# ScalarE instead of VectorE writes the placing matrix (both layers) and the last-edge coefficients (layer 1)

## The reference, cut to what matters

```
h = relu(layernorm(x));  x = x + layer0(h)      # tensor products of h[src] with edge attributes, summed by dst
h = relu(layernorm(x));  x = x + layer1(h)
# layer1: c    = w_comp[etype]                      16 coefficients an edge
#         a    = tanh(relu(sum(x_hat * y_hat) / sqrt(32)))   attention of an edge
#         nei  = segment_sum(a * sum_b c_b * (h[src] @ weight_b), dst)
#         curr = h[src[last edge of the node]] @ self_loop_weight
#         relu(nei + curr)
```

## Time and profile before

| | us |
|---|---|
| median of 3 runs (3200.29 to 3203.24) | 3202.84 |
| the profiled execution, its own time | 3200.61 |
| its span, first to last instruction | 3198.8 |
| PE busy | 3075.6 (96%) |
| VectorE busy | 2687.4 (84%) |
| POOL busy | 2333.2 (73%) |
| ScalarE busy | 779.6 (24%) |

### The profile page before, as it was taken

One profiled execution on the slowest core, in us unless ns is written; L12 is line 12 of the kernel. 1 busy time (PEld: TensorE's weight loads), 2 busy tenths in 40 slices (PEclk: granted clock), 3 DMA queues, 4 the chain that ended last, 5 costly groups with the idle time before them and its releaser, 6 DMA issues.

```text
span 3198.8 us, 112293 instructions
## 1 busy us (share of the span) xinstructions
PE 3075.6 (96%) x44682; PEld 2741.8 (86%) x44682; DVE 2687.4 (84%) x4152; ACT 779.6 (24%) x1648; POOL 2333.2 (73%) x2461
## 2 busy tenths in 40 slices
PE   2999999999999999999699999999999999999998
PEld 2888888888888888888589989898988988999997
DVE  7777777777777777777589999999999999999996
ACT  2000000000000000000343434343433343333442
POOL 6777777777777777777477777777777777777774
PEclk9999999999999999999699999999999999999998
DMA  4111111111111111111233333333333333333232
GB/s 141 32 28 29 29 28 28 29 29 29 29 29 29 29 28 28 28 29 31 74 61 59 56 59 57 59 56 59 57 59 55 60 57 59 55 60 59 56 65 47
DMA packets 217720, 151.05 MB, mean 47 GB/s; under 512 B 121592, under 2 KB 198349, under 8 KB 217167
## 3 DMA queue, kind: packets, MB, share of 16 engines
q1 hardware_dynamic: 137999, 100.77, 12.7%
q0 software_dynamic: 78592, 40.40, 12.0%
q10 hardware_dynamic: 576, 2.40, 0.2%
HBM read 135.13 MB, written 8.22 MB: 45 GB/s over the span
## 4 chain that ended last, share of the span: by engine, by line
PE 75%; DVE 14%; issue 7%; DVEq 2%; ACT 1%; DMA 0%; ACTq 0%
PE ps L625 51%; PE ps L651 10%; PE ps L682 8%; DVE blocks L946 4%; PE ps L664 3%; DVE scratch L955 3%; DVE room L1025 2%; PE ps L638 2%; DVE dots L996 1%; DVE xg L960 1%; DVE squares L993 1%; PE ps L588 1%; DVEq L1038 1%; DVE squares L1033 1%; DVE coef L1006 1%
## 5 line engine op out<-in xcount | busy, mean ns | idle before, releaser
L553 POOL DMA_INDIRECT xg<-h_table,idx x2456 | 2322.4, 946 | 829.2 <-issue 712.9
L625 PE MATMUL ps<-h,blocks 128*128 128x448 f32 x9380 | 2048.3, 372 | 40.3 <-DVE blocks L946 37.2
L625 PEld LDWEIGHTS ps<-h,blocks 128*128 128x128 f32 x9380 | 1725.9, 188 | 202.6 <-issue 27.7
L946 DVE TENSOR_TENSOR blocks<-scratch,ps 128x896 fp32r<-128x896 int16 x670 | 722.2, 1078 | 16.6 <-issue 9.2
L1025 DVE TENSOR_TENSOR room<-coef,ps 128x756 f32<-128x756 f32 (+1 forms) x522 | 648.7, 1284 | 5.0 <-DVE ps L966 0.2
L955 DVE SCALAR_TENSOR_TENSOR scratch<-ramp_sb,scratch,ps 128x448 f32<-128x448 f32 x670 | 452.1, 675 | 172.7 <-PE ps L625 170.5
L819 ACT ACTIVATE p_left<-ps 32x168 f32<-32x168 f32 (+1 forms) x262 | 78.6, 300 | 1774.4 <-PE ps L682 1763.9
L682 PEld LDWEIGHTS ps<-room,xg 128*32 128x32 f32 x25008 | 370.6, 110 | 86.3 <-issue 75.5
L682 PE MATMUL ps<-room,xg 128*32 128x28 f32 (+3 forms) x25008 | 431.1, 209 | 14.0 <-issue 9.4
L960 DVE TENSOR_REDUCE xg<-scratch 128x32 f32<-128x448 f32 x670 | 415.5, 620 | 24.4
L651 PEld LDWEIGHTS ps<-w_sb,p_left 128*84 128x84 f32 (+1 forms) x2610 | 243.6, 153 | 28.0 <-ACT p_left L820 3.5
(11 more groups left out here) (102 smaller groups left out, 837.3 us busy)
## 6 DMA issues: line engine op xcount, KB each, us to landing
xg<-h_table,idx POOLq DMA_INDIRECT x2456
rows_b<-typ_short SPq DMA_DIRECT2D x130, 258.0 KB
scratch<-q_short SPq DMA_DIRECT2D x260, 96.0 KB
rows_b<-dst_short SPq DMA_DIRECT2D x130, 126.0 KB
coef<-in_edge_dram SPq DMA_DIRECT2D x130, 54.0 KB
att_tab<-p_table SPq DMA_DIRECT2D x393, 8.1 KB
p_table<-room SPq DMA_DIRECT2D x8, 297.0 KB, 3.6
X<-in_x_dram SPq DMA_DIRECT2D x7, 224.0 KB, 4.9
```

Of the source, the lines that this page charges most:

```text
L553: pool.indirect_dma_start(xg[:, g.q, t - g.s * J, :], None, h_table[n], bass.IndirectOffsetOnAxis(ap=idx[:, t:t + 1], axis=0)).then_inc(L. ...
L625: last = pe.matmul(found_ps[b], blocks[:, b, c, :], h_2[:, a, c], start=(c == 0 and a == 0), stop=(c == NCH - 1 and a == 1))
L946: dve.tensor_tensor(blocks[:, b], q_b[:, g.b, i, :].unsqueeze(1).broadcast_to([P, NCH, P]), block_ps.unsqueeze(2).broadcast_to([P, NCH, P] ...
```

## The change

ScalarE gets two new functions, and VectorE loses `last_edges` and the last part of `spread`. ScalarE writes `R` as it makes the one-hot rows: Abs of `place - n` for each of the two halves, then Relu of one minus that over both, in place, behind a wait on a new semaphore `off_set`. It does so at the end of step t for group t-1, and in layer 1 it copies the last-edge coefficients of group t just before. `iota_row` is the ramp in SBUF; VectorE had read it from PSUM (`iota_ps`). Some waits are added ahead of the loops on ScalarE, since `R` shares memory with the tile `squares`.

```
 # ScalarE, edge_copies
+                def last_edges(g):
+                    b, nj = g.b, g.nj
+                    tiles = slice(FULL * J, T) if g.tail else bass.ds(g.s * J, J)
+                    wait(act, L.Z_set, g.order() * 2 - 4)
+                    act.activation(coef1[:, b, 0:nj, NBASE], last_all[:, tiles], ACT.Copy).then_inc(L.last_set, 1)
+
+                def placing(g):
+                    hh, w = g.halves()
+                    wait(act, L.placed, g.order() - 2)
+                    for h in range(hh):
+                        at = place[0:w, FULL, h:h + 1] if g.tail else place[0:w, bass.ds(g.s, 1), h]
+                        act.activation(R[0:w, g.b, h, :], iota_row[0:w, :], ACT.Abs, bias=at, scale=-1.0)\
+                           .then_inc(L.off_set, 3 - hh)
+                    act.wait_ge(L.off_set, g.order() * 2)
+                    act.activation(R[0:w, g.b, 0:hh, :], R[0:w, g.b, 0:hh, :], ACT.Relu, bias=1.0, scale=-1.0).then_inc(L.R_set, 1)
...
                     if n == 1 and gs[1]:
                         attention(gs[1])
+                    if n == 1 and gs[0]:
+                        last_edges(gs[0])
+                    if gs[1]:
+                        placing(gs[1])
...
+            act.wait_ge(high_set, NCH)
+            act.wait_ge(consts_in, 16)
+            act.wait_ge(windows_set, 11)
             edge_copies(0)
...
+            act.wait_ge(high_set, 2 * NCH)
+            act.wait_ge(split_set, 2 * NCH)
             act.wait_ge(p_set, NU)
             edge_copies(1)
 # VectorE, edge_work
-                def last_edges(g):
-                    b, nj = g.b, g.nj
-                    wait(dve, L.Z_set, g.order() * 2 - 4)
-                    one = iota_ps[:, 1:2]
-                    dve.tensor_tensor(coef1[:, b, 0:nj, NBASE], tiles(last_all, g), one.broadcast_to([P, nj]), ALU.mult)\
-                       .then_inc(L.last_set, 1)
...
-                    hh, w = g.halves()
-                    wait(dve, L.placed, o - 2)
-                    at = place[0:w, FULL, 0:hh] if g.tail else place[0:w, bass.ds(g.s, 1), :].rearrange("p a h -> p (a h)")
-                    dve.tensor_tensor(R[0:w, b, 0:hh, :], at.unsqueeze(2).broadcast_to([w, hh, P]),
-                                      iota_ps[0:w].unsqueeze(1).broadcast_to([w, hh, P]), ALU.is_equal)\
-                       .then_inc(L.R_set, 1)
...
-                    if n == 1 and new:
-                        last_edges(new)
```

More of the change, by code:

```diff
@@ L377, in __init__ @@
                 self.Z_set = sem(f"Z_set{n}")
+                self.off_set = sem(f"off_set{n}")
                 self.R_set = sem(f"R_set{n}")
@@ L836, in step @@
                         attention(gs[1])
+                    if n == 1 and gs[0]:
+                        last_edges(gs[0])
+                    if gs[1]:
+                        placing(gs[1])
                 def one_pass(k):
-                    if n == 1 and not isinstance(k, int):
+                    if not isinstance(k, int):
                         act.wait_ge(L.moved_on, k * (2 + 2 * n))
```

## The result

The changed kernel takes 3186.08 us in the median of four runs (3184.47 to 3187.71), the kernel before 3201.57 us in four runs beside them (3200.19 to 3203.24): ratio 0.9951, 95% interval 0.9939 to 0.9963. The profiled execution took 3186.35 us (span 3184.4, clock 0.984), where that of before took 3200.61: 14.3 us less. Forecast were 13.8 us less (3186.8 us) for that execution and a median of 3189 us, in a range from 3181 to 3198.

A forecast was written before the change was run, and what follows sets the result against it. POOL was taken to bound layer 0 and PE layer 1, with VectorE close behind. 0 + 17.4 - 4.0 + 0.4 = 13.8 us off 3200.6 gave 3186.8, median 3189, range 3181 to 3198.

The forecast's parts named there:

- Layer 0, 0 us: Layer 0: POOL's gathers bound it and VectorE idles, so the lighter VectorE gains 0 us.
- Start of layer 1, 0.4 us: Start of layer 1: PE's 0.41 us of idle time there is given back, 0.4 us gained.
- Loop, 17.4 us of excess: Eight turns of VectorE's loop in layer 1: they exceed PE's own pace by 17.4 us, which a lighter VectorE can recover.
- The 10.1 us put down to small latenesses between the ends: Layer 1 loop, steps between turns' ends: 10.1 us of the excess, wiped out by 0.54 us less VectorE work a step.
- Of it 4.0 us stay at the turns' ends: Layer 1, seven turns' ends: PE's branch stalls of 7.3 us give back 3.3 us and 4.0 us stay.
- The predicted 0.47 us by which the branch moves up: Each turn's end in layer 1: the branch comes 0.47 us earlier, from 0.12 us of sequencer work and 0.35 us at L1006.
- ScalarE's 1.4 to 1.7 us in cover: ScalarE in layer 1: 1.4 to 1.7 us added a step, covered by 5.34 us idle before copy_G, costing nothing.
- The tails, 0 to 0.5 us: Ends of the layers: 0, at most 0.5 us lost each, where placing of group 130 stands before its copy_G.
- the rival with the free turn's end: Layer 1 turns' ends: the branch stalls vanish too because the turn gets shorter, gain 17.8 us, 3185 us; chance 0.32.
- The chain as the cause: Layer 1: find, project, copy_o, attention, L1006 and Z set the pace, not VectorE's load; gain 6 us, 3197; chance 0.15.
- further table load: ScalarE before Tanh: switching function tables each step costs 1.28 us a load, some 65 us in all, 3268; chance 0.05.
- The signs: Trace checks: layer 1's copy_G 1163 us apart, PE idle 2 to 5 us, layer 0's end within 0.5 us, VectorE 76 us less busy.

The follow-up runs named there:

- e3: Kernel before with ScalarE writing R in layer 0 only, layer 1 as before; 0.7 us of difference in the median against the kernel before.
- the load put back: Changed kernel with VectorE also doing its two old instructions into buffers nobody reads; 3195.80 us against 3203.83 for the kernel before, ratio 0.9976.
- e11: Kernel before with VectorE doing the is_equal of the placing matrix twice in both layers; 27 us more than the kernel before (+0.55%).
- the last experiment: The run with VectorE's two old instructions put back into the changed kernel, for nobody; 3195.80 us, ratio 0.9976 against the kernel before.
- e8: The full change once more, on a chip where the kernel before takes over 4700 us; ratio 0.9876 against the kernel before.
- e7: Changed kernel with three more copies on ScalarE per step of layer 1, 5.7 us a step; faster than the kernel before, ratio not in the text.
- e6: Changed kernel with the last-edge copy given back to VectorE, so only R is moved; its two runs gained 12 and 15 us against the kernel before.

## Why the prediction was right

*Layer 0, 0 us.* Right: POOL's rows didn't change. e3 adds less than it seems to, since POOL waits for PE there.

*Start of layer 1, 0.4 us.* `copy_G` of group 0 came 0.8 us earlier (1620.66 against 1621.47), but at group 10 only 0.1 us was left of it. No gain from here in the end.

*Loop, 17.4 us of excess.* Right, and now with a cause in VectorE's own step: 24.31 us a pair against PE's 24.15, plus the turns' ends. The 10.1 us put down to small latenesses between the ends were there: PE's stalls of over 0.2 us outside the seven turns' ends add up to 6.7 us before and 0.5 after, and the rest of the 10.1 us is not in stalls of that length. That the gain would be the excess and not the 52 us freed was right too. What the forecast didn't see is that the excess is the loop's own: written out, VectorE's two-tile step is 0.45 us shorter.

*Of it 4.0 us stay at the turns' ends.* This is the term that was mis-sized. PE's seven stalls were 7.7 us before (7.3 forecast) and 1.0 are left of them, not 4.0; the turns as a whole kept 1.3 us of excess. The place of the earlier trace rows, one turn's end, VectorE in the kernel after:

```profile
2019.41 0.36 DVE L1026 TENSOR_TENSOR coef<-ps,att 128x192 f32<-128x192 f32 x1 [0.22 <-ACT att L795]
2019.81 3.19 DVE L1045 TENSOR_TENSOR room<-coef,ps 128x1428 f32<-128x1428 f32 x2
2024.05 1.09 DVE L974 TENSOR_TENSOR blocks<-scratch,ps 128x896 fp32r<-128x896 int16 x1 [1.05 <-issue]
```

The chain of waits there, kernel after:

```profile
2019.89 0.06 DVEq L179
...
2023.81 0.09 DVEq L179
```

and PE behind it:

```profile
2025.19 0.47 PE L626 MATMUL ps<-h,blocks 128*128 128x448 f32 x1 [0.60 <-DVE blocks L974]
```

From the branch to the sequencer's next instruction it is 3.92 us, before 4.29. Over the seven turns of layer 1 the mean fell from 3.94 to 3.43 us. The predicted 0.47 us by which the branch moves up came (it stood 0.98 us behind the end of the attention and stands 0.51 behind it), and 0.51 us of fetch came off as well: 7 x 0.98 = 6.9 us of the 7.3, and PE's wait here fell from 1.43 to 0.60 us. I had taken the fetch as fixed. With the load put back it is 3.90 us again. The number of VectorE's records in a turn is 529, 480 and 528 in the three kernels, so it goes with the length here (469 were forecast for the change); on the other chips it doesn't (2.82 to 2.92 us at 480 to 541 records, and 3.29 in layer 0 of e11 at 454). Why is open.

*ScalarE's 1.4 to 1.7 us in cover.* Right: Abs 0.39 us (0.38 forecast), Relu 0.42, copy 0.22 (0.20). The idle time ahead of `copy_G` in the step of the earlier trace rows went from 5.34 us to 4.11, L1026 waits for ScalarE's attention as foreseen, and PE doesn't wait for ScalarE in the turns. The rule of the Trainium skill that was weighed ("ScalarE: Activation LUTs", "Rules for kernel authors": relu and add go to VectorE) holds for the busy time, which more than doubled for the same values; the measured ratio says that it doesn't decide where ScalarE idles.

*The tails, 0 to 0.5 us.* Too small, and for another reason than the one forecast. Group 128 still comes 15.8 us ahead of before; then 1.4 us are lost between `copy_G` and `copy_o` of group 129, in PE's 20 matmuls of `project`. Busy time in this stretch (columns as in the earlier trace rows), first the kernel before,

```profile
3171.30:3174.40 3.10, 2.02 (x20) 1.79 (x20) 0.00 (x0) 0.96 (x3) 0.00 (x0) 1.00 0.00 0
```

then the kernel after.

```profile
3155.60:3160.00 4.40, 3.42 (x20) 3.09 (x20) 0.00 (x0) 0.90 (x2) 0.00 (x0) 0.50 0.00 0
```

The granted clock (the column before the last two) is 1.00 before and 0.50 after, that is 2.4 and 1.2 GHz, and the same 20 matmuls take 3.42 us instead of 2.02. Both kernels had fallen to the lower clock a little before, each in an idle time of PE of over 1 us: the kernel before at 3167.7 us, ahead of the `sum_edges` that starts at 3168.02, the kernel after at 3149.9, ahead of the `attention_rows` that starts at 3150.55, some 2 us earlier in its tail. The kernel before had the full clock again from 3171.1 to 3174.5 us, which is this stretch, the kernel after never. What decided that was not tried. `placing` of group 130, which the forecast had named, comes only behind.

*The sum.* Forecast 13.8; measured in the profiled executions 0.1 (to group 10) + 16.1 (turns) - 0.4 (to group 127) - 1.5 (tail) = 14.3. Two errors of opposite sign, 2.7 us in the turns and 1.5 us in the tail, nearly cancel, so that the sum comes within 0.5 us is luck in part. The median was forecast as 3189 and is 3186.08: the 2.2 us by which the median before lay over its profiled execution were carried over, and the kernel after has its median 0.3 us below. The 3185 of the rival with the free turn's end is thus nearer than the forecast's own 3189.

*The rivals.* That the turn's end comes free nearly came true in its time, but not for its reason. Its evidence was misread: "shows no stall from the branch" in layer 0 is not so. The branch at 592.1 is followed by the sequencer's next instruction at 594.99, and L946 starts 0.24 us behind that, at 595.23, just as in layer 1 (2027.75 and 2027.98). The 0.86 us of idle time ahead of it are the end of a fetch, though the row names PE as the releaser, and the same holds at all seven turns' ends of that layer. The fetch takes 2.87 us there in the mean (2.82 after); it costs nothing since VectorE has time to spare in layer 0. The fetch did not end at 480 records a turn either, where the page "Advanced Engine Details and Errata", section "ISA Cache", of the Trainium skill gives room for 512 instructions; the trace doesn't bear out a limit at 512 recorded instructions. The chain as the cause fell with the last experiment. No further table load was seen: there is one within the layers' edges, as before.

*The signs.* The two `copy_G` stand 1160.6 us apart (1163 forecast), PE idles 2.0 us in the turns (2 to 5), and layer 0 ends 0.3 us later (within 0.5). VectorE's busy time in layer 1 fell by 59 us, from 1467.7 to 1408.4, and not by 76.

## What to carry to other kernels

Measure each engine's own period over the repeating pattern of steps, from a point that doesn't wait to the next. Where an engine's period is a little above the bounding engine's, work taken off it is worth the difference, times the number of periods, and nothing beyond; it may cost more than twice the time on an engine that idles. A branch at the end of a turn is a term of its own, and how much of it shows depends on how long an instruction covers it. Compare the same step inside and outside a hardware loop too: here the loop's register work made VectorE the slower engine.

## What the runs showed of the hardware

- The kernel before takes 3202 us on some chips and 4730 to 4838 on others. VectorE's, ScalarE's and POOL's busy times are the same to 0.5%; PE's is 3612 us in the change again (e8) against 3074.7, at a mean granted clock of 0.857 against 0.984, and it idles for want of its own instructions. The granted clock in the turns of e8, busy time by stretch:

```profile
2439.00:4287.00 1848.00, 1366.08 (x18374) 1214.56 (x18374) 1066.85 (x1493) 572.29 (x1248) 860.39 (x912) 0.84 0.23 37
```

- Whether there is a fetch behind the branch of a turn went with the length of the turn in these runs. On ScalarE a turn of 298 records goes on 0.23 us after the branch (e8), one of 337 records, with the ballast (e7), 2.5 us after it, and one of 273 on e7's chip 0.24 us (e6); on SP 122 records need 0.3 to 0.9 us in the mean and 399 2.5 to 2.7; VectorE with 418 to 541 records always has the fetch, 2.8 us or more in the mean. Instructions of ScalarE's queue in e7 at two turns' ends (first and last start us):

```profile
L179 ACTq COMPARE_BRANCH  x2: 45/45/45, 3900.4 to 4142.7; - x2
L179 ACTq FUSED_REGOPS  x2: 50/50/50, 3902.8 to 4145.2; - x2
```

So a turn that is cut to under some 300 records on VectorE might lose its fetch; it was not tried.
